# Expert layers of a graph network: each node's row goes to its two experts in pages of 256 slots, and edge sums are made node tile by node tile

## What is computed

```
h = x @ W_in + b_in
for l in range(L):
    agg = segment_sum(h[src], dst) / deg
    logits = concat([h, agg]) @ router_W[l] + router_b[l]        # 8 logits
    vals, idx = top_k(logits, 2); gates = softmax(vals)
    gate_dense = zeros.at[rows, idx].set(gates)
    weak   = relu(agg @ weak_W[l] + weak_b[l])                   # 4 x [256, 256]
    sh     = relu(agg @ strong_W1[l] + strong_b1[l])             # 4 x [256, 512]
    strong = sh @ strong_W2[l] + strong_b2[l]                    # 4 x [512, 256]
    moe = einsum('ne,neh->nh', gate_dense, concat([weak, strong]))
    h = h + sigmoid(h @ conf_W[l] + conf_b[l]) * moe
return h @ W_out + b_out
```

## Time and profile before

| what | value |
|---|---|
| runs, median of 3 | 3159.76 us (3158.73 to 3162.07) |
| profiled execution: its span (the profile gives no other time of it) | 3158.2 us |
| PE busy | 2940.0 us, 93% |
| DVE busy | 2182.3 us, 69% |
| ACT busy | 942.8 us, 30% |
| POOL busy | 16.7 us, 1% |
| expert block, from the end of relations (1612.6) to the end | 1545.6 us |

### The profile page before, as it was taken

One profiled execution on the slowest core, in us unless ns is written; L12 is line 12 of the kernel. 1 busy time (PEld: TensorE's weight loads), 2 busy tenths in 40 slices (PEclk: granted clock), 3 DMA queues, 4 the chain that ended last, 5 costly groups with the idle time before them and its releaser, 6 DMA issues. The chain is left out here.

```text
span 3158.2 us, 47679 instructions
## 1 busy us (share of the span) xinstructions
PE 2940.0 (93%) x18758; PEld 1775.7 (56%) x18758; DVE 2182.3 (69%) x4012; ACT 942.8 (30%) x1776; POOL 16.7 (1%) x23
## 2 busy tenths in 40 slices
PE   2888889999998999999989999989999999999997
PEld 1566555556454544544556666655666665666665
DVE  7999565557346777776667666777767677766676
ACT  3888522113211000000032222343323234323223
POOL 2000000000000000000000000000000000000000
PEclk8899999999999999999989999999999999999999
DMA  5445367776006554554330000020000002000001
GB/s 130 141 142 160 107 188 211 218 232 198 23 1 204 154 171 153 166 156 129 93 117 4 4 4 4 3 84 4 4 7 4 3 21 67 4 4 4 4 3 43
DMA packets 310959, 265.85 MB, mean 84 GB/s; under 512 B 32767, under 2 KB 289409, under 8 KB 308174
## 3 DMA queue, kind: packets, MB, share of 16 engines
q1 hardware_dynamic: 296558, 259.28, 27.0%
q10 hardware_dynamic: 13760, 2.61, 0.4%
q0 software_dynamic: 416, 0.85, 0.1%
HBM read 172.67 MB, written 90.05 MB: 83 GB/s over the span
## 5 line engine op out<-in xcount | busy, mean ns | idle before, releaser
L1948 PE MATMUL psum<-r_wd,room_a 128*128 128x512 fp8e4 (+1 forms) x2600 | 569.5, 375 | 1.0 <-ACT r_ht L286 1.0
L2526 PE MATMUL psum<-counts,m_h 128*128 128x512 fp8e4 (+2 forms) x2100 | 417.9, 355 | 13.5 <-DVE m_h L2241 8.0
L2590 PE MATMUL psum<-m_weights,x_nodes 128*128 128x256 f16 (+1 forms) x3600 | 415.4, 273 | 12.5 <-DVE m_wtmp L2349 10.2
L2571 PE MATMUL psum<-room_a,m_weights 128*128 128x512 f16 (+2 forms) x2016 | 411.5, 356 | 14.6 <-ACT x_nodes L2481 8.6
L1948 PEld LDWEIGHTS psum<-r_wd,room_a 128*128 128x128 f16 x2600 | 241.7, 97 | 295.9 <-ACT r_ht L286 1.1
L2590 PEld LDWEIGHTS psum<-m_weights,x_nodes 128*128 128x128 f16 (+1 forms) x3600 | 352.1, 99 | 65.1 <-DVE m_wtmp L2349 9.6
L2473 ACT ACTIVATE m_agg<-psum,x_nodes 128x512 f32<-128x512 f32 (+2 forms) x336 | 239.4, 718 | 292.9 <-PE psum L2571 290.1
L2526 PEld LDWEIGHTS psum<-counts,m_h 128*128 128x128 f16 x2100 | 206.0, 99 | 208.9 <-issue 11.5
L2571 PEld LDWEIGHTS psum<-room_a,m_weights 128*128 128x128 f16 x2016 | 193.7, 99 | 214.5 <-issue 40.2
L2493 ACT ACTIVATE m_hT<-m_hT,room_a 128x256 f32<-128x256 f32 x300 | 135.7, 500 | 553.4 <-DVE m_hT L2363 553.4
L2349 DVE SCALAR_TENSOR_TENSOR m_wtmp<-psum,x_nodes,room_a 128x256 f32<-128x256 f32 (+1 forms) x300 | 144.8, 483 | 137.9 <-PE psum L2590 136.5
(11 more groups left out here) (311 smaller groups left out, 3381.2 us busy)
## 6 DMA issues: line engine op xcount, KB each, us to landing
r_wd<-packed_sym SPq DMA_DIRECT2D x120, 640.0 KB, 4.1
packed_counts<-strip SPq DMA_DIRECT2D x21, 1800.0 KB, 7.8
sym_blocks<-packed_counts SPq DMA_DIRECT2D x88, 384.0 KB, 4.8
packed_sym<-sym_blocks SPq DMA_DIRECT2D x84, 384.0 KB, 3.6
w_stage<-in_L_gnn_strong_W SPq DMA_DIRECT2D x12, 1024.0 KB, 6.6
m_weights<-in_L_gnn_strong_W SPq DMA_DIRECT2D x21, 512.0 KB, 4.7
x_parked<-x_nodes SPq DMA_DIRECT2D x2, 1600.0 KB, 5.9
x_nodes<-x_parked SPq DMA_DIRECT2D x2, 1600.0 KB, 6.3
```

Source lines behind the costliest of these rows:

```text
L1948: m = pe.matmul(bank[pair[b]][:, 0:2 * cw], h16[:, part, p0 + i, :], f_[:, 2 * b:2 * b + 2, :], start=(p0 + i == 0 and part == 0), stop=(p ...
L2526: m = pe.matmul(bank[kb][:, 0:cw], h16[:, part, i, kb * P:(kb + 1) * P], A[:, i, c_:c_ + cw], start=(i == 0 and part == 0), stop=(i == NT ...
L2571: m = pe.matmul(bank[4 + hh % 2][:, 0:cw], w_[:, i, kb, f * P:(f + 1) * P], agg16[:, j, kb, 0:cw], start=(x_ == 0), stop=(x_ == len(todo) ...
L2590: m = pe.matmul(bank[b_][0:r_, 0:H], s_[:, pa[0] * BANK + k * P:pa[0] * BANK + k * P + r_], w_[:, pa[1], f, :], start=(f == 0 and pa == PA ...
```

## The change

`block_experts` is rewritten; everything ahead of it keeps its order, but for small additions in the relations stage (the biases of the weak experts are loaded and join the maxima; 1/deg is loaded by node tile; POOL clears semaphores to free their numbers).

**Edge sums node tile by node tile.** The counts of 128 source by 128 destination nodes are stationary now, and all 512 columns of a source tile's h (256 high, 256 low) move. A destination tile is 25 such matmuls in one PSUM bank (`edge_tiles`), nodes on partitions. The first six destination tiles (HEAD) share each source tile as it becomes ready, the other 19 follow one by one. `mean` adds high and low, applies 1/deg, and splits the row into float16; SP stores the rows (1 KB each) in a DRAM table `agg_rows`. PE turns h and the mean for the logits (4 transposes).

**Routing.** In eight runs of 1, 4, 4, 4, 4, 4, 3 and 1 tiles (RUNS): `choose` finds the two experts on DVE, `ranks` counts on PE how many nodes ahead chose the same expert, `assign` gives each choice a slot (page and place in it) in 32 further DVE operations. POOL scatters, for each tile and choice, 128 entries of 16 bytes (node, destination row, code of the weights) into a list in DRAM, by indirect DMA. After the last, SP loads the list back.

**Pages.** 32 pages of 256 slots. For each page POOL gathers 2 x 128 rows of `agg_rows`, up to four pages ahead (GR = 4); PE turns them (8 float16 transposes); PE and DVE load the page's code into a register; PE makes the hidden layer and the output with the weights at an address from that register, 24 + 24 matmuls of 256 columns; a page of two weak experts uses an identity as second matrix. POOL scatters the 2 x 128 result rows (1 KB each) into a DRAM table by node and choice. At the start of the next layer (and of the output) SP loads this table and DVE adds both rows of each node, times their gates, to h (`dve_combine`), tile by tile ahead of the split and the edge sum.

```diff
+    PG = 2 * P
+    PAGES = (2 * N + NE * (PG - 1)) // PG
+    ORD = [NT - 1] + list(range(NT - 1))
+    HEAD = 6
+    CUTS_R = [0, 1, 5, 9, 13, 17, 21, NT - 1, NT]
+    def turned_in(k):
+        a = 2 * (k - HEAD)
+        return [t for t in (a, a + 1) if t < k] if a < k - 1 else [k - 1]
...
+            def pool_layer(l):
...
+                    for t in range(n_):
+                        for k in range(2):
+                            pool.indirect_dma_start(out=slot_lists[l], out_offset=bass.IndirectOffsetOnAxis(ap=at_list[0:r_, c_ % 2, k, t:t + 1], axis=0),
+                                                    in_=put[0:r_, k, i0 + t, :], in_offset=None).then_inc(list_out[c_ % 2], 16)
...
+                for j in range(GR):
+                    gather(j)
+                for j in range(PAGES):
+                    for s in range(SUB):
+                        pool.wait_ge(p_y, (l * PAGES + j) * SUB + s + 1)
+                        pool.indirect_dma_start(out=y_rows[l], out_offset=bass.IndirectOffsetOnAxis(ap=fld[:, j * SUB + s, 1:2], axis=0),
+                                                in_=ysb[j % 2][s], in_offset=None).then_inc(y_out[j % 2], 16)
+                    gather(j + GR)
...
+            def dve_layer(l):
...
+                scales()
+                if l == 0:
...
+                        low(i)
+                else:
+                    dve_combine(l, low)
+                more_scales()
+                for k in range(NT):
+                    if k >= HEAD:
+                        for t in turned_in(k - 1) if k > HEAD else ():
+                            if run_ending(t) is not None:
+                                assign(run_ending(t))
+                                if run_ending(t) < len(RUNS) - 2:
+                                    gates(run_ending(t))
+                        for t in turned_in(k):
+                            if run_ending(t) is not None:
+                                choose(run_ending(t))
+                    mean(k)
+                    if HEAD + 2 <= k < HEAD + 2 + NPC:
+                        split_low(k - HEAD - 2)
+                last = len(RUNS) - 1
+                assign(last - 1)
+                choose(last)
+                assign(last)
...
+                at = page_of(0)
+                hidden(0, at)
+                for j in range(PAGES):
+                    if j + 1 < PAGES:
+                        next_at = page_of(j + 1)
+                        hidden(j + 1, next_at)
+                    outputs(j, at)
...
+            def pe_layer(l):
...
+                def turn(t):
+                    pe.wait_ge(e_mean, n + 1)
...
+                def page_of(j):
+                    v = pe.value_load(fld[0:1, j * SUB, 2:3], min_val=0, max_val=8 * MOST + NBI - 1)
+                    return pe.snap((v & 7) * (2 * SL)), pe.snap((v >> 3) * H)
...
+                def hidden(j, first):
...
+                                w_ = w16[:, bass.ds(first + (SPECIAL * H + part * SL + kb * BANK + f * P), P)]
+                                for y_ in range(2 - part):
+                                    m = pe.matmul(o_, w_, x[:, y_, kb, :], start=(kb == 0 and part == 0 and y_ == 0),
+                                                  stop=(kb == KB - 1 and part == 1))
...
+                for k in range(HEAD, NT):
+                    ts = turned_in(k)
+                    edge_tiles(k, range(0, 6))
+                    turn(ts[0])
+                    edge_tiles(k, range(6, 12))
+                    logits(ts[0])
+                    edge_tiles(k, range(12, 18))
+                    if k > HEAD:
+                        for t in turned_in(k - 1):
+                            if run_ending(t) is not None:
+                                ranks(run_ending(t))
+                    for t in ts[1:]:
+                        turn(t)
+                    edge_tiles(k, range(18, NT))
+                    for t in ts[1:]:
+                        logits(t)
...
+                for j in range(PAGES):
+                    if j + 2 < PAGES:
+                        turn_page(j + 2)
+                    if j + 1 < PAGES:
+                        hidden(j + 1, next_at[0])
+                    outputs(j, at[1])
...
```

More of the change, by code:

```diff
@@ new lines, in block_experts @@
+            place = sbuf(c, "m_place", [P, 2, LT, NE], F32)
+            slot_of = [sbuf(c, f"m_slot_of{i}", [P, LT, NE], F32) for i in range(2)]
+            sm = sbuf(c, "m_sm", [P, 2, 10, LT], F32)
+            slots = sbuf(c, "m_slots", [P, 2, 2, LT], F32)
+            at_list = sbuf(c, "m_at_list", [P, 2, 2, LT], I32)
+            packs = sbuf(c, "m_packs", [P, NE], F32)
+            pages = sbuf(c, "m_pages", [P, 14, NE], F32)
+            new_pages = beside[:, 4 * SLOTS + 8 * NT:4 * SLOTS + 8 * NT + 3 * (NE + 4)].bitcast(F32).rearrange("p (k e) -> p k e", k=3)
@@ new lines, in block_experts, with scale_of, ring_uses, gathers @@
+            oT = [room_a[:, i * H:(i + 1) * H].rearrange("p (k n) -> p k n", n=P) for i in range(2)]
+            k_hidden, k_strong = ks[:, 4:5], ks[:, 5:6]
+            HALVES = (slice(0, SL // 2), slice(SL // 2, SL))
+            def scale_of(l, k, of):
+                t = 0 if k < NPR + NSG else 1
+                return of[:, t * NLAY + l:t * NLAY + l + 1]
+            def ring_uses(r, ring, upto, each):
+                return sum(each for k in range(upto) if k % ring == r)
+            def gathers(l, j):
+                r = j % GR
+                return 16 * (l * ring_uses(r, GR, PAGES, SUB) + ring_uses(r, GR, j + 1, SUB))
@@ new lines, in dve_layer @@
+                scales()
+                if l == 0:
+                    vec.wait_ge(parked, 16)
+                    for i in range(NT):
+                        low(i)
+                else:
+                    dve_combine(l, low)
[13 more added lines that the diff above has]
+                        split_low(k - HEAD - 2)
@@ new lines, in dve_layer @@
+                last = len(RUNS) - 1
+                assign(last - 1)
+                choose(last)
+                assign(last)
+                gates(last - 1)
+                gates(last)
+                vec.wait_ge(list_in, 16 * (l + 1))
+                at = page_of(0)
[5 more added lines that the diff above has]
+                    outputs(j, at)
+                    at = next_at
```

1190 lines of the change are left out of this document (652 added, 538 removed).

## The result

The changed kernel takes **3230.01 us** (3227.19 to 3236.05, 4 runs) against 3159.49 us: ratio **1.0221**, 95% interval 1.0207 to 1.0236, slower by 2.2%. Forecast were 3116 us and a probable gain. The profiled execution has a span of 3225.4 us, 110.8 above the sum's 3114.6.

The account below looks back on a forecast made before the run. The prediction took PE to bound the kernel. Layers of 479, 487 and 487 us plus output 49 made 1502 against 1545.6 us, a span of 3114.6 and a median of 3116 us; range 3040 to 3240, the forecast's own 3040 to 3153.

Parts of the forecast that it names:

- the sum: Expert block, all terms added: 1502 against 1545.6 us, 44 us less, so a profiled span of 3114.6 us.
- D: The pages of a layer: 32 at 6.72 us (6.42 from the queues, 0.3 for registers), 215 us.
- E: Between layers and at the end: 12 us twice from a layer's last matmul, output 49 us, start 9 us.
- the output: After the last layer: 49 us instead of 31.6, with 25 tiles on DVE taking 29 us of it.
- A: First edge tiles of a layer, 25 source tiles by six matmuls: 33 us in the first layer, 38 in the others.
- B: The other 19 edge tiles of a layer: 141 us of PE work and 40 of waits, 181 us.
- C: From a layer's last edge matmul to its first page, with nothing else for PE: 33 us.
- F: PE's clock: 1.1 us for each restart at the low level, about seven a layer, 8 us a layer.
- the forecast's own range: Whole kernel without the rivals: 3040 to 3153 us, with a chance of 0.58.
- Rival 1: Pages: PE's queue, with its register load and register operations, becomes the bound; 7.6 us a page, 3200 us; chance 0.17.
- Rival 2: Pages: POOL's indirect DMAs each wait for a DVE operation; 7.8 us a page, 3230 us; chance 0.07.
- Rival 3: DVE's chain of choose and assign weighs more in the edge tiles and before the pages; 3197 us; chance 0.06.

Follow-up runs that it names:

- e16: The changed kernel, unaltered, measured again on the fifth chip: 3151.5 us, ratio 0.9974 to the kernel before.
- e5: Changed kernel with the pages' gathers and scatters as plain DMAs on SyncE's queue, rows in order instead of by the lists: 3045.7 us.
- e3: Changed kernel with PE loading no register in the pages and using one fixed piece of weights; DVE keeps its registers: 3205.1 us.
- e18: e17 with one piece of the experts' weights loaded behind each store of summed rows, instead of all ahead; fifth chip: 2964.2 us, ratio 0.9381.
- e17: Changed kernel with gathers ahead of scatters and paced, DVE's mean before assignment, output bias added once; fifth chip: 2976.2 us, ratio 0.942.

## Why the prediction was right or wrong

- **The failed step is in D: "Laying the queues out by these durations gives 6.42 us a page."** It supposed that an engine's update arrives when its work ends. In the first measurement it didn't, for more than one update in four, and the page stages took 246, 245 and 240 us instead of 215. Where updates were prompt they took 227, 220 and 217 us, and D with E was 11 and 4 us over the forecast instead of 30 and 28. Of the 111 us that the profiled span lies over the sum, 71 go with the late updates (3225.4 against 3154.2 us). The other 40 are, in `e16`, 32 in the last layer's pages and the output, 15 in D and E of the first two layers and 13 in A, less 19 in B, C and F and 1 ahead of A. So without hold-ups the sum would still have been off by 35 us of median time, and the forecast's own range, up to 3153 us, would have held by 2 us. That the whole range, up to 3240 us, holds 3230 is luck.
- **D's other parts held.** PE's own page is 5.7 us (5.94 forecast; the small matmuls of the earlier trace rows from which 0.54 us for the transposes came are bf16, not float16, and the transposes take 0.45), indirect DMAs beside DVE work take 0.99 to 1.04 us on the mean, within the forecast's 0.94 to 1.33, and `e5` needs no 0.3 us for register operations.
- **Rival 1**, PE's queue as the bound, is refuted: with all its registers PE made pages 5.7 us apart in `e5`, without them (`e3`) the changed kernel still took 7.12. The trace has the register load as

```profile
L2806 PEldq TENSOR_LOAD <-m_b x31: 295/301/388, 2388.8 to 2621.9; - x31
```

0.30 us each. The Trainium skill (DMA: Bandwidth & Descriptors, "Latency and other measured facts") gives such a load a floor of about 600 ns; by the trace it is half of that, and beside the matmuls of `e5` it costs nothing.

- **Rival 2** gave 3230 us, the very number, by a mechanism that did not occur: POOL's instructions stayed at 1.0 us beside DVE's. The interference shown goes another way, from POOL to PE's semaphores. The Trainium skill (SBUF — State Buffer, "Who interferes with whom") speaks of the port that DVE and POOL share; no row here shows POOL slowed by it.
- **Rival 3** did not occur: B, C and F together were 13 us under the forecast over three layers. But that is two errors of opposite sign. C, from the last edge matmul to the first page, took 25.7 to 25.8 us in each layer against 33: its items in the prediction add up to 31, not 33, and were together too high besides. B with F took 187, 193 and 195 us against 189. There the mechanism was right: four waits a layer on the mean, 4.3 us each instead of 5.1, and in the first layer three on ACT of 4.8, 1.7 and 3.5 us instead of 5, 3 and 4. Two of them, logits (L2775) behind ACT and a turn (L2760) behind a mean (L2448):

```profile
1664.96 0.89 PE L2775 MATMUL psum<-m_rw,m_edge_room 128*53 128x9 f32 x8 [4.80 <-ACT m_edge_room L2675]
...
1726.31 0.69 PE L2760 MATMUL psum<-ident,room_b 128*128 128x128 f32 x2 [4.29 <-DVE m_edge_room L2448]
```

In layers 2 and 3 the first of the three waits is 10.5 and 11.1 us, not 5: the first stores of summed rows land 9.4 and 9.0 us after issue, behind 5 MB of weights on SP's queue, as the chain of waits has it:

```profile
2171.78 9.37 DMA agg_rows<-m_edge_room
...
2687.37 9.04 DMA agg_rows<-m_edge_room
```

The forecast let nothing queue there; loads between stores are worth 12 us (`e18` against `e17`).
- **F** (8 us a layer for the clock) may be too small. In B PE waits for 30, 37 and 38 us (40 forecast) and is busy for 157, against 141 of work at the full rate, at a granted clock of 0.87 to 0.88. How much of the 16 us is the clock no run separates.
- **A was too low by 15 us**, most of it not the clock. In the first layer:

```profile
1616.56 20.64 PE L2850 MATMUL psum<-room_a,counts 128*53 128x512 f16 x72 [2.54 <-DVE room_a L2396]
1637.13 18.25 PE L2850 MATMUL psum<-x_nodes,counts 128*53 128x512 f16 x72
```

The first 72 run at a granted clock of 0.87, the restart that the forecast put into F. The next 72 run at 1.00 and still take 0.25 us each instead of 0.22: of the six matmuls of each source tile the first stands 0.31 us behind the matmul ahead of it and 0.33 ahead of the next, the others 0.22 apart. The two semaphore waits ahead of each source tile stand there, and `edge_tiles`, which has none between its matmuls, keeps to 0.22; no run takes them away to show that it is they. That is 5 of the 7 us by which A missed in this layer.
- **The output was the second large miss**, 29 of the 57 us in the last line of the table. The stretch from its first transposes on is 65.3 us; the forecast had 36.5 for it (49 less 12.5 of waiting), taking DVE's 1.14 us a tile as its pace. PE paces it: busy for 57.7 of 65.3 us, 2.3 us a tile, at a granted clock of 0.50, the level of 1.2 GHz, after a wait of 14 us and with small matmuls alone. That PE may be the slower side there was never worked out.

Of the 463 us saved on PE, the sum said that 420 come back. Without hold-ups it was 456 (3158.7 less 3151.5 is what remains), in the first measurement 533.

## What to carry over

Lay out the queues of all engines before moving work off a bound engine, and give each stage its own slowest engine again, the small ones at the low clock too: here the queue order on DVE (56 us), on POOL and SP, and one pair of small matmuls a tile (18 us) were worth more than the change itself, and with them it reaches 0.938 of the time before. Where a profile shows an engine starting microseconds after its releaser's end with "remote" beside it, look at when the semaphore was raised, and avoid long unbroken rows of indirect DMAs on POOL. A result that rests on them must be measured on more than one chip, and more than once.

## What was unexpected of the hardware

In three sets of five, each on its own chip, rows of POOL's indirect DMAs (0.85 to 1.0 us each, 0.3 us apart) kept back PE's semaphore updates: by up to 2.5 us in the changed kernel's pages, by up to 4 us and more where the gathers go ahead, and in a row of 96 so that they came through one each 16 to 17 us, which took 116 us from a kernel that had nothing to do with the DMAs. Rows, bytes and DMA load did not matter (122 us at a DMA share of 0.03), and single ones with 1.5 us between cost nothing. In the two other sets the same page loops ran with no late update, which makes the same program 2.4% faster there.
